# Attention and routed experts on one core: router logits taken from the first normalised tile and the output projection, and routing two blocks behind instead of three

## The reference

```python
x = x + xattn(layernorm(x), ctx)          # x, ctx: 128 x 128 x 256; 16 heads of 16
x = x + ffn(layernorm(x))

def ffn(x):                               # 32 experts, hidden width 64
    logits = x_flat @ router_w.T + router_b
    routed_idx = argmax(logits)
    h = relu(x_flat @ w1[e] + b1[e])      # e = routed_idx of the token
    return relu(h @ w2[e] + b2[e])
```

## Time and profile before

| | us |
|---|---|
| median of three runs | 1224.18 (1223.42 to 1226.62) |
| the profiled execution | 1223.15 |
| its span, first to last instruction | 1221.3 |
| TensorE busy | 1097.5 (90%) |
| VectorE busy | 925.0 (76%) |
| ScalarE busy | 858.5 (70%) |
| GpSimd busy | 847.3 (69%) |

### The profile page before, as it was taken

The page is one execution under the profiler, slowest core; times in us unless marked ns, Lnnn a source line. Parts: engine busy times, 40 slices in busy tenths (PEclk is TensorE's granted clock), DMA queues, the critical chain, the costliest instruction groups (busy, mean ns, idle before and its releaser), DMA issues.

```text
span 1221.3 us, 39225 instructions
## 1 busy us (share of the span) xinstructions
PE 1097.5 (90%) x15399; PEld 845.1 (69%) x15399; DVE 925.0 (76%) x2321; ACT 858.5 (70%) x2020; POOL 847.3 (69%) x1613
## 2 busy tenths in 40 slices
PE   5999999999999999999999999999998419998893
PEld 4777777777777777777777777777776319977772
DVE  4787888888888888888888888888877427866772
ACT  4777777777777777777777777777776306655551
POOL 4544777677777777777777777777764656777776
PEclk9999999999999999999999999999999859999997
DMA  7415222522222222222222222222110136676650
GB/s 243 147 56 121 71 72 71 142 80 76 76 73 79 82 83 75 80 71 72 72 78 74 72 71 72 71 72 72 59 41 29 52 132 205 198 215 205 205 161 17
DMA packets 91156, 120.40 MB, mean 99 GB/s; under 512 B 14096, under 2 KB 73883, under 8 KB 90781
## 3 DMA queue, kind: packets, MB, share of 16 engines
q1 hardware_dynamic: 77150, 84.04, 24.2%
q0 software_dynamic: 13824, 33.85, 7.7%
HBM read 60.61 MB, written 59.31 MB: 98 GB/s over the span
## 4 chain that ended last, share of the span: by engine, by line
PE 60%; DVE 20%; POOL 7%; DMA 5%; issue 4%; ACT 3%; SPq 1%; POOLq 0%; DVEq 0%; ACTq 0%
PE pB L832 10%; PE pA L774 9%; PE pB L824 8%; PE sc L782 7%; DVE mx L595 6%; PE sc L806 5%; POOL out L419 4%; PE sc L765 4%; PE sc L815 3%; ACT arena L468 3%; DVE nrm L621 3%; PE m L791 3%; PE sc L1000 3%; DMA out<-arena 2%; PE m L798 2%
## 5 line engine op out<-in xcount | busy, mean ns | idle before, releaser
L595 DVE TENSOR_REDUCE mx<-m 128x4 bf16<-128x512 f32 x512 | 322.6, 670 | 10.7 <-PE m L791 10.5
L468 ACT ACTIVATE arena<-sc 128x512 f32<-128x512 f32 x512 | 264.5, 603 | 47.5 <-PE sc L815 47.5
L419 POOL DMA_INDIRECT out<-arena x160 | 157.0, 981 | 60.9 <-issue 31.1
L615 DVE STREAM_TRANSPOSE tr<-pB 128x512 f32<-128x512 f32 x128 | 91.8, 717 | 106.3 <-PE pB L824 106.3
L806 PE MATMUL sc<-qk 32*128 32x256 f32 x2048 | 167.0, 397 | 0.5 <-DVE rbp L674 0.5
L824 PE MATMUL pB<-arena 128*32 128x128 f32 x4096 | 159.8, 276 | 1.5 <-issue 1.0
L386 POOL DMA_INDIRECT pages<-row,slot_i x128 | 130.4, 1019 | 40.0 <-issue 37.0
L832 PE MATMUL pB<-wo_s,aT 128*128 128x256 f32 x512 | 138.0, 392 | 8.7 <-DVE aT L626 8.7
L824 PEld LDWEIGHTS pB<-arena 128*32 128x32 f32 x4096 | 99.0, 109 | 44.6 <-issue 43.6
L774 PE MATMUL pA<-cHi,wqkv 128*128 128x512 f32 x252 | 119.0, 474 | 9.4 <-DVE wqkv L660 9.4
L774 PE MATMUL pA<-xnT,wqkv 128*128 128x512 f32 x372 | 124.7, 443 | 0.0
(11 more groups left out here) (141 smaller groups left out, 2714.9 us busy)
## 6 DMA issues: line engine op xcount, KB each, us to landing
arena<-pages SPq DMA_DIRECT2D x160, 130.0 KB
cT<-ctxT SPq DMA_DIRECT2D x64, 256.0 KB, 3.8
xs<-x_in SPq DMA_DIRECT2D x128, 128.0 KB, 3.3
pages<-empty SPq DMA_DIRECT2D x120, 130.0 KB, 3.1
pages<-empty SPq DMA_DIRECT2D x1, 5200.0 KB, 19.8
out<-arena POOLq DMA_INDIRECT x160
w2s<-w SPq DMA_DIRECT2D x1, 2080.0 KB
qk<-w SPq DMA_DIRECT2D x1, 2064.0 KB, 8.2
```

Source lines behind the costliest of these rows:

```text
L419: pool.indirect_dma_start(out_rows, bass.IndirectOffsetOnAxis(pr[:, r, COL_TOKEN:COL_TOKEN + 1].bitcast(U32), 0), pr[:, r, 0:D], None, bou ...
L468: act.activation(pt[:, u % 2, g].rearrange("p i k -> p (i k)"), sc[g][:, :], ACT.Exp).then_inc(S["exp_out"], 1)
L595: ins = dve.tensor_reduce(mx[:, 32 * g:32 * g + 4], mb[i][:, :].rearrange("p (h k) -> p h k", h=4), AX.X, ALU.max)
L615: dve.transpose(tr[:, :], pB[:, :]).then_inc(S["tr_out"], 1)
```

## The change

The mean-subtracted, scaled row of the second norm is linear in x and in the attention output, apart from the factor rstd. So the logits of the second norm are rstd times (x @ Wc + attention @ Wo @ Wc) plus bias, where Wc is the router's matrix with the mean over features taken out (so that no mean has to be subtracted), and with the mean over experts taken out (so that the 32 logit columns add nothing to the row sum that `residual` accumulates; the argmax doesn't change by it). The change computes:

- in setup: Wc, the product of Wo's transpose with Wc as 32 more columns of `wo_s`, and the output bias times Wc as 32 more of `bo_s` (`mean_router`, `output_bias`, `router_weights`, `router_bias` on TensorE, four matching steps on VectorE);
- `logits(s + 1)` at u = 1 from xnTf, the transposed first normalised tile in full precision. It is kept for this: ScalarE now copies PSUM to xnTf and then xnTf to xnT (`xnT_copy`), and `xnT_lo` subtracts from xnTf. `x_logits` multiplies by the standard deviation (`sd1`, a new operation in `rstd1`) and writes the columns 256 to 287 of xs;
- a `project_out` of 288 columns, and `add_bo` and `residual` of 288;
- `scale_logits`: two GpSimd operations, times rstd and plus router bias.

`norm2`, the transposes of xn2, their copies and `logits_across` go. `rstd2` is one call for four batches. Routing of block s − 1 is finished in block s up to `place`, and scattered at the start of block s + 1. In GpSimd's loop slot_i and the scatters now come first. `choose`, `scan`, `slot_sum` and some of the statistics move on VectorE to a place behind `maxima`. The context loads are issued at u = 1 and 2. The four columns with token, expert, mean and rstd move to the front of a row; its length in the pages stays 260.

```diff
-        wo_s = sb("wo_s", [2, D])
+        wo_s, won_s = sb("wo_s", [2, D + E]), sb("won_s", [2, D])
+        mean_w, shift_e = sb("mean_w", [P]), sb("shift_e", [2])
...
+                    if u in (1, 2) and live(q + 3):
+                        load_ctx(q + 3, u - 1)
...
-                r, m, g = rs1[:, q % 2, :], nm1[:, q % 2, :], ag1[:, q % 2]
+                r, m, v, g = rs1[:, q % 2, :], nm1[:, q % 2, :], vr1[:, q % 2, :], ag1[:, q % 2]
                 after(pool, "agg1_out", 4, q, 3)
                 if q >= 2:
                     after(pool, "xn_out", 2, q - 2, 1)
-                pool.tensor_scalar(r, g[:, :, 1], EPS, None, ALU.add).then_inc(S["var1_out"], 1)
+                    after(pool, "lg_out", 1, q - 2, 0)
+                pool.tensor_scalar(v, g[:, :, 1], EPS, None, ALU.add).then_inc(S["var1_out"], 1)
                 after(pool, "var1_out", 1, q, 0)
-                pool.tensor_tensor(r, r, half[:, :], ALU.pow).then_inc(S["pow1_out"], 1)
+                pool.tensor_tensor(r, v, half[:, :], ALU.pow).then_inc(S["pow1_out"], 1)
                 after(pool, "pow1_out", 1, q, 0)
                 pool.tensor_tensor(m, g[:, :, 0], r, ALU.mult).then_inc(S["mr1_out"], 1)
+                pool.tensor_tensor(sd1[:, q % 2, :], v, r, ALU.mult).then_inc(S["std1_out"], 1)
...
-            def rstd2(q, h):
-                r, m = row[:, q % 4, 2 * h:2 * h + 2, COL_RSTD], row[:, q % 4, 2 * h:2 * h + 2, COL_MEAN]
-                after(pool, "sq_out", 4, q, 2 * h + 1)
+            def rstd2(q):
+                r, m = row[:, q % 4, :, COL_RSTD], row[:, q % 4, :, COL_MEAN]
+                after(pool, "sq_out", 4, q, 3)
...
+            def scale_logits(q):
+                if q == 0:
+                    pool.wait_ge(S["ld_b"], 80)
+                after(pool, "rstd2_out", 1, q, 0)
+                if q >= 1:
+                    after(pool, "eq_out", 1, q - 1, 0)
+                pool.tensor_tensor(lg[:, :, :], row[:, q % 4, :, X0 + D:X0 + D + E],
+                                   row[:, q % 4, :, COL_RSTD].unsqueeze(2).to_broadcast([P, QB, E]), ALU.mult).then_inc(S["scaled_out"], 1)
+                after(pool, "scaled_out", 1, q, 0)
+                pool.tensor_tensor(lg[:, :, :], lg[:, :, :], rb_s[:, :].unsqueeze(1).to_broadcast([P, QB, E]), ALU.add).then_inc(S["z_out"], 1)
 
             def add_bo(q):
                 if q == 0:
-                    pool.wait_ge(S["bo_out"], 1)
+                    pool.wait_ge(S["bo_out"], 2)
                 after(pool, "xn_out", 2, q, 1)
-                pool.tensor_tensor(xs[:, q % 4], xs[:, q % 4], bo_s[:, :].unsqueeze(1).to_broadcast([P, QB, D]),
+                after(pool, "lg_out", 1, q, 0)
+                pool.tensor_tensor(xs[:, q % 4], xs[:, q % 4], bo_s[:, :].unsqueeze(1).to_broadcast([P, QB, D + E]),
                                    ALU.add).then_inc(S["xb_out"], 1)
...
-            for s in range(-1, NQ + 3):
+            for s in range(-1, NQ + 2):
+                if live(s - 2):
+                    slots_as_integers(s - 2)
+                    scatter(s - 2)
                 if live(s - 1):
-                    rstd2(s - 1, 0)
-                if live(s - 3):
-                    place(s - 3)
+                    rstd2(s - 1)
+                    scale_logits(s - 1)
                 if live(s + 2):
                     rstd1(s + 2)
                 if s >= 0 and live(s + 2):
                     split(s + 2)
-                if live(s - 3):
-                    slots_as_integers(s - 3)
                 if live(s + 1):
                     add_bo(s + 1)
-                if live(s - 3):
-                    if live(s - 1):
-                        after(pool, "sq_out", 4, s - 1, 3)
-                    scatter(s - 3)
                 if live(s - 1):
-                    rstd2(s - 1, 1)
-                if live(s - 2):
-                    meta(s - 2)
-                    fresh_pages(s - 2)
+                    meta(s - 1)
+                    fresh_pages(s - 1)
+                    place(s - 1)
...
+                at = slice(2 * P * h, 2 * P * (h + 1))
                 after(act, "xnT_done", 2, q, h)
-                act.activation(xnT[:, 0, :, 2 * P * h:2 * P * (h + 1)], xnT_bank(q, h)[:, :].rearrange("p (c t) -> p c t", c=2),
-                               ACT.Copy).then_inc(S["xnT_out"], 1)
-
-            def xn2T_copy(q, h):
-                after(act, "xn2T_done", 2, q, h)
-                act.activation(xn2T[:, :, 2 * P * h:2 * P * (h + 1)], xn2T_bank(h)[:, :].rearrange("p (c t) -> p c t", c=2),
-                               ACT.Copy).then_inc(S["xn2T_out"], 1)
+                if q >= 1:
+                    after(act, "xnTl_out", 2, q - 1, h)
+                act.activation(xnTf[:, :, at], xnT_bank(q, h)[:, :].rearrange("p (c t) -> p c t", c=2), ACT.Copy).then_inc(S["xnTf_out"], 1)
+                after(act, "xnTf_out", 2, q, h)
+                act.activation(xnT[:, 0, :, at], xnTf[:, :, at], ACT.Copy).then_inc(S["xnT_out"], 1)
...
-                dve.scalar_tensor_tensor(row[:, q % 4, u, 0:D], pB[:, 0:D], 1.0, xs[:, q % 4, u, :], ALU.mult, ALU.add,
+                dve.scalar_tensor_tensor(row[:, q % 4, u, X0:X0 + D + E], pB[:, 0:D + E], 1.0, xs[:, q % 4, u, :], ALU.mult, ALU.add,
                                          accum_out=row[:, q % 4, u, COL_MEAN:COL_MEAN + 1]).then_inc(S["x2_out"], 1)
...
-                dve.tensor_tensor(lo, xnT_bank(q, h)[:, :].rearrange("p (c t) -> p c t", c=2), hi.bitcast(F32),
+                dve.tensor_tensor(lo, xnTf[:, :, 2 * P * h:2 * P * (h + 1)], hi.bitcast(F32),
                                   ALU.subtract).then_inc(S["xnTl_out"], 1)
...
+            def x_logits(q):
+                after(dve, "lgT_done", 1, q, 0)
+                after(dve, "std1_out", 1, q, 0)
+                if q >= 4:
+                    after(dve, "x2_out", 4, q - 4, 3)
+                dve.tensor_tensor(xs[:, q % 4, :, D:D + E], sc[3][:, 0:P].rearrange("p (u e) -> p u e", e=E),
+                                  sd1[:, q % 2, :].unsqueeze(2).to_broadcast([P, QB, E]), ALU.mult).then_inc(S["lg_out"], 1)
+
             def best(q):
-                after(dve, "lg_out", 1, q, 0)
+                after(dve, "z_out", 1, q, 0)
...
+                    if u == 0 and live(s - 2):
+                        slot_sum(s - 2)
+                    if u == 2 and live(s - 1):
+                        choose(s - 1)
+                    if u == 3 and live(s - 1):
+                        scan(s - 1)
+                    if u < 2 and live(s + 3):
+                        stats1(s + 3, (u,))
                     if live(q1):
                         attended(q1, u1)
                         normalise(q1, u1)
...
+                    if u == 1 and s >= 0 and live(s + 1):
+                        x_logits(s + 1)
                     if live(q1):
                         residual(q1, u1)
...
-                    if live(s + 3):
-                        if u == 0:
-                            stats1(s + 3, (0,))
-                        if u == 2:
-                            stats1(s + 3, (1, 2))
-                        if u == 3:
-                            stats1(s + 3, (3,))
-                    if u == 0 and live(s - 3):
-                        slot_sum(s - 3)
-                    if u == 1 and live(s - 2):
-                        best(s - 2)
-                        choose(s - 2)
-                    if u == 3 and live(s - 2):
-                        scan(s - 2)
+                    if s == -1:
+                        (centre_router, output_bias, router_weights, router_bias)[u]()
+                    if u == 1 and live(s - 1):
+                        best(s - 1)
+                    if u == 2 and live(s + 3):
+                        stats1(s + 3, (2, 3))
...
-                    ins = pe.matmul(pB[:, 0:D], aT[:, i, :], wo_s[:, i, :], start=(i == 0), stop=(i == 1))
+                    ins = pe.matmul(pB[:, 0:D + E], aT[:, i, :], wo_s[:, i, :], start=(i == 0), stop=(i == 1))
...
-                    if u == 0 and live(s - 2):
-                        if live(bq_):
-                            after(pe, "proj_out", 4, bq_, bn)
-                        after(pe, "xn2T_out", 2, s - 2, 1)
-                        if s == 2:
-                            pe.wait_ge(S["ld_wr"], 16)
-                        logits(s - 2)
+                    if u == 1 and s >= 0 and live(s + 1):
+                        after(pe, "proj_out", 4, bq_, bn)
+                        after(pe, "xnTf_out", 2, s + 1, 1)
+                        logits(s + 1)
...
-                    if u == 1 and live(s - 1):
-                        if live(s):
-                            after(pe, "exp_out", 16, s, 4 * u)
-                        after(pe, "xn2_out", 2, s - 1, 0)
-                        transposes(s - 1, 0, xn2, "xn2T_done")
...
+                        (mean_router, output_bias, router_weights, router_bias)[u]()
```

(19 more changed lines are left out.)

241 lines of the change are left out of this document (123 added, 118 removed).

## The result

The changed kernel took **1277.5 us** in the median of four runs (1267.0 to 1288.6), the kernel before 1223.8. The ratio is **1.035 (95% interval 1.033 to 1.038)**, 43 us in absolute numbers by the same interval's centre. What lowers the clock here is part of what follows. Forecast were 1257 us and a range of 1203 to 1286.

What follows compares the result with a forecast made beforehand. TensorE, busy 90%, bounds the kernel, with waits on other engines. Blocks go from 29.26 to 28.14 + 0.9 + 1.7 = 30.7 us: 29 blocks +42.9, ends −9.1, so +33.8 on 1223.15: 1257 us, range 1203 to 1286.

Steps and rivals of the forecast that it cites:

- The late ScalarE and `best` under cHi: Into slot S2: ScalarE 0.6 us late after waiting for `rstd1`, and 0.3 more as `best`'s comparison meets cHi: +0.9 a block.
- The holds: In S2, VectorE's pick product held by cLo and `hot` by the add of `bo`: +1.7 us a block.
- the slack: In S2, delay on VectorE's way to aT that TensorE would not feel: 1.2 − 0.44 + 0.9 = 1.65 us.
- The base of 28.14: A block's time if nothing new is late, from 29.26 us now: 28.14 us.
- −0.77 for `choose`: VectorE: `choose` goes behind the maxima, into the gap before PV is done: −0.77 us a block.
- −0.5 for the nrm collision: VectorE in S1: nrm no longer meets the add of `bo`, which moves to S2: −0.5 us a block.
- The other terms: Per block: transposes −0.88, exp wait +0.27, logits' transpose wait +0.13, wider output projection +0.43, double xnT copy +0.2 us.
- (d): Rival: more is caught, nrm behind the add or the next maxima; blocks of 31.7, 1286 us; chance 0.08.
- the tail: Chain after the last residual, to the fourth scatter: 17.3 us against 31.8 now, −14.4 us.
- (a): Rival: everything new covered, `choose` not held, `rstd1` in time; blocks of 28.1, 1182 us; chance 0.19.
- (b): Rival: only ScalarE's wait costs; blocks of 29.0, 1208 us; chance 0.15.
- (c): Rival: one of `choose`'s two products held; blocks of 29.8, 1231 us; chance 0.13.

Runs made afterwards that it cites:

- memset run: Changed kernel with GpSimd's add of `bo` replaced by a memset of about its length, which reads nothing from SBUF: 1198.9 us, ratio 0.978.
- add-last run: Changed kernel with GpSimd's add of `bo` moved from ahead of `meta` to behind `place`: 1234.1 us, ratio 1.008.
- the version whose holds are all covered: Changed kernel with the context split moved behind `meta`, `rstd1` a block ahead before `place`, and the add of `bo` behind `place`: 1184.2 us, ratio 0.967.
- the reordered version: Changed kernel, split behind `meta`, `rstd1` a block ahead, add behind `place`: 1184.2 us; with `rstd1(3)` behind block 0's add: 1181.7 us.
- four pieces: Changed kernel with cLo and the add of `bo` each issued as four GpSimd instructions, order unchanged: 1187.4 us, ratio 0.970.

## Why the prediction was right, and where it was not

**The mechanism** was the forecast one, in its place: S2 the long slot, pick held by cLo (1.2 us forecast, 1.33 in an ordinary block), `hot` by the add (2.5 forecast, 2.31), TensorE waiting for aT. The memset run shows that it is the read of SBUF, the add-last run that the path loses 2.02 us by `hot`. The block at full clock is 30.5 us against 30.7.

**Its split between terms** was less good. The late ScalarE and `best` under cHi were to cost 0.9; the second distance is 7.58 against 7.31 without either: 0.27. That is the comparison in `best` alone, held for 0.33; in the six blocks where it took 0.87 instead of 0.62 the distance is 7.84. ScalarE's wait of 1.15 us for rstd1 passed on nothing that shows: the mxT copy at 354.47 was late by 0.1, not 0.6. The holds were to cost 1.7 and cost 2.27 (9.54 against 7.27): 0.25 for pick and 2.02 for `hot`. The step that failed is ScalarE's lateness and with it the slack, 1.65: 0.9 of it was to come from ScalarE's lateness, which hardly existed, and what remains, 0.75, is about what the runs show (1.04 + 2.02 of hold, 2.27 of it passed on). The two errors cancel in the block, 2.54 measured for 2.6, and that is not all luck: a lateness that isn't there takes its slack away too.

**The base of 28.14** was met at 27.97 by the version whose holds are all covered. The two large terms of VectorE are confirmed apart from each other: −0.77 for `choose` is −0.78, and −0.5 for the nrm collision is −0.52 or −0.51 by the blocks in which nrm wasn't held. The kernel before with both gone would be at 28.0. The other terms together were +0.15, and from 28.00 to 27.97 they are −0.03. In single distances more moves: against 7.25, 6.59, 7.13 and 7.03, that version has 0.56 less, 0.72 more, 0.14 more and 0.33 less. Which of the terms (transposes, exp wait, wide projection, double copy) makes up the difference wasn't measured apart.

**What the sum lacked** is the clock. TensorE's waits were priced at their own length. In the profiled run they cost 32.4 us more in 17 blocks, since TensorE comes back at the lower level; even by the faster runs the kernel is at 1267, and 1262 with its waits filled. Without these 32.4 us the profiled run would be at 1254, for 1257 forecast. That all of the lowered clock still fits into the range owes something to luck: its upper part was there for (d), more holds, and the profiled run, 1286.4, is at its very edge. The prediction has no word on the clock: in before the clock line stands at 9 up to 946 us, in block 31, with single waits of 1.0 us, and nothing there shows two waits of 0.8 and 1.4 us with 0.4 us of work between them.

**The ends**: the tail was right to 0.4 us (17.7 for 17.3), block 0 was +0.9 for +1.5, the setup +4.8 for +3, inside its 0 to 6 (other runs of the same setup begin the first copy anywhere from 33.4 to 38.5, so this term is uncertain by itself). Block 30 was +2.8 for +0.8, by the hold of `best` under the add, which the prediction didn't list.

**The rivals.** (a), everything covered at 1182 us, with the condition "if the GpSimd operations from cHi on run after `hot` is written", is what the reordered version does: 1184 and 1182 us. So the change with its products free is worth 3 to 4%, 1.8% of which the kernel before gets by moving `choose` alone, and the order of GpSimd's queue took all of it away and 3.5% more. (b), only ScalarE's wait, was too dear in any case: the wait is nearly free. (c), one of the two products held, was put at 29.8; the memset run is that case with pick held, and takes 28.7, since the slack covers most of pick's hold.

## What to carry to other kernels

List each VectorE product with two inputs in SBUF and lay it beside each GpSimd operation that reads SBUF for over a microsecond; when an edit moves either queue, the list is to be read again for all of them, since here every shift freed one product and caught another (`hot`, pick, `best`, `xnT_lo`). Fix the phase by a dependence (a small operation that waits for the product's result, ahead of the long one) or cut the long one in pieces where it can't be fixed. And price a wait of TensorE with what its clock does behind it: when two waits stand close together, measure whether the clock holds, and fill one with dummy products if it doesn't.

## What the runs showed of the hardware

- A product of 0.29 us took up to 2.3 us under a GpSimd add, 1.3 under a difference and 0.6 under a cast, all of which read SBUF, and its 0.29 under a memset of 2.22 us. The hold ends with the instruction (the short products end 0.14 or 0.15 us behind it), and between two pieces VectorE gets in at once (0.38 for 0.28). That four pieces don't lock it out was new to me.
- Two waits of TensorE, 0.77 and 1.36 us, with 0.4 us of work between them, brought the granted clock to 0.58 in a stretch of 5 us; the projection behind them took 2.29 instead of 1.24 us, and a block 1.3 or 2.6 us more. It happened in 17 of 29 blocks in one execution, with the same waits in all. Three products of 256 columns in the second wait, with the first left at 0.78, stopped it in all of them. The Trainium skill describes such a clock gate, with a window that runs free of the program (TensorE: Matmul & The Clock Gate, Part 1); blocks alike in their waits and unlike in their clock agree with that, but no run here tests it.
